# Two graph convolutions: node rows as three exact bfloat16 parts, three bfloat16 products per item, and a ring of 16 slots instead of 24

## The reference, cut to what matters

```python
def _gcn_conv(x, src, dst, W, b):
    h = x * (deg_out ** (-0.5))[:, None]
    h = h @ W
    m = segment_sum(h[src], dst, num_segments=N)
    return m * (deg_in ** (-0.5))[:, None] + b
h = relu(_gcn_conv(layernorm(x), src, dst, W1, b1))
x = x + _layer_norm(_gcn_conv(h, src, dst, W2, b2), gamma, beta)
```

## Time and profile before

| what | value |
|---|---|
| median of 3 runs | 5920.07 us (5916.95 to 5927.35) |
| profiled execution | 5863.58 us |
| its span in the trace | 5861.9 us |
| mean granted clock of TensorE | 0.793 of full |
| busy: PE, PEld, DVE, ACT, POOL | 66%, 48%, 44%, 16%, 50% |
| p1's items, about | 2897 to 4119 us |
| c1's tile loop, about | 4122 to 4189 us |
| p2's items, about | 4204 to 5399 us |

### The profile page before, as it was taken

One profiled execution on the slowest core, in us unless ns is written; L12 is line 12 of the kernel. 1 busy time (PEld: TensorE's weight loads), 2 busy tenths in 40 slices (PEclk: granted clock), 3 DMA queues, 4 the chain that ended last, 5 costly groups with the idle time before them and its releaser, 6 DMA issues.

```text
span 5861.9 us, 62152 instructions
## 1 busy us (share of the span) xinstructions
PE 3845.1 (66%) x14313; PEld 2804.7 (48%) x14313; DVE 2575.1 (44%) x7839; ACT 966.5 (16%) x2299; POOL 2943.7 (50%) x2860
## 2 busy tenths in 40 slices
PE   1666667777788799999355555554655555556368
PEld 0333335566667588888233333333433333334257
DVE  8433234555576511111244444445444444445841
ACT  5333232222102522222200000000200000000421
POOL 0666665565300033333366666667266666664513
PEclk9777778888898799999667767666767776767669
DMA  2333335565687344444433333332233333332202
GB/s 78 106 105 108 105 106 178 185 195 186 198 254 235 107 109 115 111 109 110 140 88 93 91 92 92 92 92 80 81 91 92 92 92 92 92 92 84 88 16 32
DMA packets 322621, 660.17 MB, mean 113 GB/s; under 512 B 60683, under 2 KB 142923, under 8 KB 322150
## 3 DMA queue, kind: packets, MB, share of 16 engines
q0 software_dynamic: 148960, 365.25, 21.4%
q1 hardware_dynamic: 152870, 253.42, 14.4%
q10 hardware_dynamic: 20448, 37.52, 2.1%
HBM read 488.94 MB, written 174.87 MB: 113 GB/s over the span
## 4 chain that ended last, share of the span: by engine, by line
PE 20%; issue 11%; DVE 10%; another core or an unknown queue 6%; DVEq 2%; DMA 1%; ACT 1%; SPq 0%; POOL 0%; POOLq 0%; ACTq 0%
PE bank L1769 15%; DVE reg_b L1313 6%; DVEq L304 2%; PE bank L1717 2%; DVE reg_a L1298 1%; PE bank L1728 1%; PE bank L1689 1%; DVEq L1313 1%; DVE small L822 0%; DVE work L1471 0%; DMA conv_rows<-work 0%; PE bank L1750 0%; DVE work L1505 0%; ACT reg_b L681 0%
## 5 line engine op out<-in xcount | busy, mean ns | idle before, releaser
L1769 PE MATMUL bank<-work,reg_a 128*128 x3520 | 1329.6, 526 | 1175.0 <-issue 626.0
L617 POOL DMA_INDIRECT work<-conv_rows,tables x1662 | 1575.8, 948 | 935.5 <-issue 482.9
L1769 PEld LDWEIGHTS bank<-work,reg_a 128*128 128x128 f32 x3520 | 821.3, 256 | 1683.2 <-issue 1570.1
L1313 DVE TENSOR_TENSOR reg_b<-reg_b,bank 128x257 f32 x1760 | 743.1, 422 | 1026.2 <-remote 518.6
L578 POOL DMA_INDIRECT messages<-work,small x880 | 884.3, 1005 | 536.3 <-ACT work L708 251.2
L1628 PE MATMUL bank<-reg_b,reg_a 128*128 x1760 | 602.8, 477 | 427.6 <-issue 191.1
L1298 DVE TENSOR_SCALAR reg_a<-iota,tables 128x128 f32<-128x128 f32 x1760 | 553.7, 315 | 274.9 <-issue 197.5
L1628 PEld LDWEIGHTS bank<-reg_b,reg_a 128*128 128x128 f32 x1760 | 363.1, 229 | 610.1 <-issue 569.8
L708 ACT ACTIVATE work<-bank,tables 128x256 f32<-128x256 f32 x880 | 397.7, 474 | 1042.5 <-PE bank L1628 630.4
L599 POOL DMA_INDIRECT residual_rows<-work,slot_t x112 | 177.9, 1589 | 478.2 <-DVE work L1282 308.3
L1641 PE MATMUL bank<-reg_b,reg_a 128*128 128x257 f32 x1544 | 395.0, 405 | 28.3 <-DVE reg_a L1164 16.3
(11 more groups left out here) (340 smaller groups left out, 3827.5 us busy)
## 6 DMA issues: line engine op xcount, KB each, us to landing
reg_b<-messages SPq DMA_DIRECT2D x316, 258.0 KB
reg_a<-in_L_ffn_W_dram SPq DMA_DIRECT2D x56, 1024.0 KB, 5.4
reg_a<-item_rows SPq DMA_DIRECT2D x110, 256.0 KB
work<-conv_rows,tables POOLq DMA_INDIRECT x1662
b_rows<-messages ACTq DMA_DIRECT2D x72, 258.0 KB
reg_b<-messages ACTq DMA_DIRECT2D x70, 258.0 KB
b_rows<-messages SPq DMA_DIRECT2D x56, 258.0 KB
messages<-work,small POOLq DMA_INDIRECT x880
```

The costliest lines, as they stand in the source:

```text
L617: g.indirect_dma_start(GC[:, u, 0:D], None, table, bass.IndirectOffsetOnAxis(ap=BSRC[:, b_:b_ + 1], axis=0)).then_inc(z(f"conv_in{u // 4}" ...
L1313: v.tensor_tensor(acc, acc, ps[i % 8][:, 0:D + 1], ALU.add).then_inc(z(f"{tag}_add"), 1)
L1769: pe.matmul(ps[i % 8][:, 0:D + 1], OHP[:, i % (2 * OHN), :], GCf[:, bass.ds(offs[i % 4], D + 1)], start=True, stop=True).then_inc(z(f"{tag ...
```

## The change

Each fp32 number of a row is stored as three bfloat16 numbers that add up to it exactly: its upper 16 bits (the head), the upper 16 bits of what is left (the middle), and what is left then (the rest). A row has 3 x 256 bfloat16 numbers, 1536 bytes instead of 1024, and a slot of the ring has 770 (with the one, and one to pad). The ring has 16 slots. The one-hots are bfloat16 too, made from a bfloat16 copy of the row of column numbers (`IOTAB`). An item is three products into the same bank: rest with the column of ones (257 columns), middle, head (256 each).

The row's producer now writes fp32 to a buffer of its own (`XF`, two chunks), and three copies fill `XR`: ACT copies the heads of a chunk (a strided read of every second 16-bit number, 1792 numbers a partition), DVE subtracts the heads from the numbers (into `XL`) and then the middles from that (the rests), ACT copies the middles from `XL`. SP waits for all three before it writes the chunk. In `c1`, a chunk's heads go at the first tile of the next chunk, its rests at the third, its middles at the fifth; the last chunk's follow the loop, and its rests stand ahead of the zeroing of `ACC`. The semaphores of one-hots, additions and ones are shared by the two convolutions.

```diff
     U = 16
-    UM = UC = 24
+    UM, UC = 24, 16
     NI = -(-(NBLK + T - 1) // U) * U
...
         x2_t = dram("residual_rows", [FPAD, D])
-        conv1_t = dram("conv1_rows", [T * P, D])
-        conv2_t = dram("conv2_rows", [T * P, D])
+        conv1_t = dram("conv1_rows", [T * P, 3 * D], BF16)
+        conv2_t = dram("conv2_rows", [T * P, 3 * D], BF16)
         xn4_t = dram("ffn_in_rows", [T * P, D])
-        WORK = 6700
+        WORK = 6640
+        PARTS = 3 * D
+        SLOT = PARTS + 2
         SMALL = 2600
...
         OHN = 4
-        OHP = ta[:, 0:2 * OHN * P].rearrange("p (s n) -> p s n", n=P)
+        OHP = ta[:, 0:OHN * P].bitcast(BF16).rearrange("p (s n) -> p s n", n=P)
         G, BOH8 = carve(0, UM * W, 2 * 222)
         G = G.rearrange("p (u w) -> p u w", w=W)
-        GCf = work[:, 0:UC * (D + 1)]
-        GC = GCf.rearrange("p (u w) -> p u w", w=D + 1)
+        GCf = work[:, 0:UC * SLOT // 2].bitcast(BF16)
+        GC = GCf.rearrange("p (u w) -> p u w", w=SLOT)
+        assert UC * SLOT // 2 <= WORK
         BOH8 = [BOH8[:, k * 222:(k + 1) * 222].bitcast(BF16)[:, 0:9 * T].rearrange("p (j t) -> p j t", t=T) for k in range(2)]
...
         assert T * D + 3 * QW <= NE * HC * D and QW <= NE * D
-        XR, XT, ZB = carve(0, 2 * CH * D, 2 * D, 2 * D)
-        XR = XR.rearrange("p (s t d) -> p s t d", s=2, d=D)
+        XR, XT, ZB = carve(0, 3 * CH * D, 2 * D, 2 * D)
+        XR = XR.bitcast(BF16).rearrange("p (s t d) -> p s t d", s=2, d=PARTS)
+        XF = ta[:, 0:2 * CH * D].rearrange("p (s t d) -> p s t d", s=2, d=D)
+        XFH = ta[:, 0:2 * CH * D].bitcast(BF16).rearrange("p (s t d k) -> p s t d k", s=2, d=D, k=2)[:, :, :, :, 1]
+        XL = B2B[:, 0:CH * D].rearrange("p (t d) -> p t d", d=D)
+        XLH = B2B[:, 0:CH * D].bitcast(BF16).rearrange("p (t d k) -> p t d k", d=D, k=2)[:, :, :, 1]
+        assert T * (D + 1) + 2 * CH * D <= NE * KC * H and CH * D <= NE * D
         XT = XT.rearrange("p (s c n) -> p s c n", s=2, c=KC)
...
             return z(f"rows_out{k}"), 16 * (before * each + (each if n is None else n))
+        PARTED = dict(p1=0, p2=NCH)
+        def parts_free(tag, c):
+            return rows_out(c % 2, 1 + CONV[tag], c // 2)
         assert EC % 2 == 0
...
             for c in range(NCH):
-                sp.wait_ge(*norms("ln3", "norm", c + 1))
+                for part in ("head", "middle", "rest"):
+                    sp.wait_ge(z(f"part_{part}"), PARTED["p1"] + c + 1)
                 sp.dma_start(nodes(conv1_t, c), XR[:, c % 2, :, :]).then_inc(z(f"rows_out{c % 2}"), 16)
...
                         pool.wait_ge(z(f"{tag}_free"), b_ - UC + 4)
-                    g.indirect_dma_start(GC[:, u, 0:D], None, table,
+                    g.indirect_dma_start(GC[:, u, 0:PARTS], None, table,
                                          bass.IndirectOffsetOnAxis(ap=BSRC[:, b_:b_ + 1], axis=0)
...
             network(**MOE)
+            def heads(tag, c):
+                if c >= 2:
+                    act.wait_ge(*parts_free(tag, c))
+                a.copy(XR[:, c % 2, :, 0:D], XFH[:, c % 2]).then_inc(z("part_head"), 1)
+            def middles(tag, c):
+                act.wait_ge(z("part_left"), PARTED[tag] + c + 1)
+                a.copy(XR[:, c % 2, :, D:2 * D], XLH).then_inc(z("part_middle"), 1)
             for c in range(NCH + 1):
...
                     if c >= 3:
-                        act.wait_ge(*rows_out((c - 1) % 2, 1, (c - 1) // 2))
-                    ln_apply("ln3", c - 1, lambda i: X[:, (c - 1) * CH + i, :], lambda i: XR[:, (c - 1) % 2, i, :])
+                        act.wait_ge(z("part_left"), c - 2)
+                    ln_apply("ln3", c - 1, lambda i: X[:, (c - 1) * CH + i, :], lambda i: XF[:, (c - 1) % 2, i, :])
+                    act.wait_ge(*norms("ln3", "norm", c))
+                    heads("p1", c - 1)
+                if c >= 2:
+                    middles("p1", c - 2)
+            middles("p1", NCH - 1)
             def releases(tag):
...
                 if c >= 2 and t % CH == 0:
-                    act.wait_ge(*rows_out(c % 2, 2, c // 2))
-                a.activation(XR[:, c % 2, t % CH, :], ZB[:, t % 2, :], ACT.Relu, scale=DO[:, t:t + 1]
+                    act.wait_ge(z("part_left"), PARTED["p2"] + c - 1)
+                a.activation(XF[:, c % 2, t % CH, :], ZB[:, t % 2, :], ACT.Relu, scale=DO[:, t:t + 1]
                              ).then_inc(z("relu1"), 1)
+                if c >= 1 and t % CH == 0:
+                    act.wait_ge(z("relu1"), c * CH)
+                    heads("p2", c - 1)
+                if c >= 1 and t % CH == 4:
+                    middles("p2", c - 1)
+            act.wait_ge(z("relu1"), T)
+            heads("p2", NCH - 1)
+            middles("p2", NCH - 1)
             releases("p2")
...
             v.tensor_copy(TRIB[:, 0, :], TRI[:])
+            v.tensor_copy(IOTAB[:], IOTA[:])
             v.memset(TRIB[:, 2, :], 1.0)
...
                         v.wait_ge(z(f"{tag}_mm"), i - 7)
-                    v.tensor_scalar(OHP[:, i % 8, :], IOTA[:], DREL[:, i:i + 1], None, ALU.is_equal
-                                    ).then_inc(z(f"{tag}_oh"), 1)
-                v.memset(GC[:, :, D:D + 1], 1.0).then_inc(z(f"{tag}_one"), 1)
+                    v.tensor_scalar(OHP[:, i % 8, :], IOTAB[:], DREL[:, i:i + 1], None, ALU.is_equal
+                                    ).then_inc(z("conv_oh"), 1)
+                v.memset(GC[:, :, PARTS:PARTS + 1], 1.0).then_inc(z("conv_one"), 1)
                 for i in range(OHN):
...
                     if i:
-                        v.wait_ge(z(f"{tag}_add"), i)
+                        v.wait_ge(z("conv_add"), CONV[tag] * NI + i)
                     acc = ACCf[:, bass.ds(offs[i % 4], D + 1)]
-                    v.tensor_tensor(acc, acc, ps[i % 8][:, 0:D + 1], ALU.add).then_inc(z(f"{tag}_add"), 1)
+                    v.tensor_tensor(acc, acc, ps[i % 8][:, 0:D + 1], ALU.add).then_inc(z("conv_add"), 1)
             v.wait_ge(z("s_add"), NPR)
...
             network(**MOE)
-            for c in range(NCH + 1):
+            def rests(tag, c):
+                n = PARTED[tag] + c
+                if n:
+                    v.wait_ge(z("part_middle"), n)
+                    v.wait_ge(z("part_rest"), n)
+                v.tensor_tensor(XL, XF[:, c % 2], XFH[:, c % 2], ALU.subtract).then_inc(z("part_left"), 1)
+                v.wait_ge(z("part_left"), n + 1)
+                if c >= 2:
+                    v.wait_ge(*parts_free(tag, c))
+                v.tensor_tensor(XR[:, c % 2, :, 2 * D:PARTS], XL, XLH, ALU.subtract).then_inc(z("part_rest"), 1)
+            for c in range(NCH + 2):
                 if c < NCH:
...
                     ln_stats("ln3", c, lambda i: X[:, c * CH + i, :])
-                if c >= 1:
+                if 1 <= c <= NCH:
                     ln_scale("ln3", c - 1, extra=DO)
+                if c >= 2:
+                    v.wait_ge(*norms("ln3", "norm", c - 1))
+                    rests("p1", c - 2)
             v.wait_ge(z("acc1_zero"), 1)
...
             item_sums("p1")
-            v.wait_ge(z("p1_add"), NI)
+            v.wait_ge(z("conv_add"), NI)
             step(v.tensor_scalar(RM, ACC[:, :, D], 1.0, None, ALU.max))
...
                 product("c1", 0, t, ZB[:, t % 2, :], GB1B).then_inc(z("lin1"), 1)
+                c = t // CH - 1
+                if c >= 0 and t % CH == 2:
+                    v.wait_ge(z("relu1"), (c + 1) * CH)
+                    rests("p2", c)
+            v.wait_ge(z("relu1"), T)
+            rests("p2", NCH - 1)
             v.memset(ACCf, 0.0).then_inc(z("acc2_zero"), 1)
...
             item_sums("p2")
-            v.wait_ge(z("p2_add"), NI)
+            v.wait_ge(z("conv_add"), 2 * NI)
             for t in range(T):
...
             def item_products(tag):
-                pe.wait_ge(z(f"{tag}_one"), 1)
+                pe.wait_ge(z("conv_one"), CONV[tag] + 1)
                 def places(i):
                     return (pe.value_load(ROW_N[:, i // 4:i // 4 + 1], min_val=1, max_val=NBLK),
-                            table_offsets(PE_, ROW_C[:, i:i + 4], (UC - 1) * (D + 1)))
+                            table_offsets(PE_, ROW_C[:, i:i + 4], (UC - 1) * SLOT))
                 after = places(0)
...
                         after = places(i + 3)
-                    pe.wait_ge(z(f"{tag}_oh"), i + 1)
+                    pe.wait_ge(z("conv_oh"), CONV[tag] * NI + i + 1)
                     if i >= 8:
-                        pe.wait_ge(z(f"{tag}_add"), i - 7)
-                    pe.matmul(ps[i % 8][:, 0:D + 1], OHP[:, i % (2 * OHN), :], GCf[:, bass.ds(offs[i % 4], D + 1)],
-                              start=True, stop=True).then_inc(z(f"{tag}_mm"), 1)
+                        pe.wait_ge(z("conv_add"), CONV[tag] * NI + i - 7)
+                    for k in (2, 1, 0):
+                        width = D + (k == 2)
```

(17 more changed lines are left out.)

## The result

The changed kernel takes 6047.14 us (median of 4 runs, 6039.5 to 6055.8) and the kernel before 5919.9 (4 runs): +127 us, ratio 1.0219 (95% interval 1.02 to 1.0238). The forecast was 6090, in a range from 5690 to 6330. The number is near; of the four terms in its sum one was right, and errors in the others cancelled. That is luck, and the last sections say where.

A forecast was written before the change was run, and what follows sets the result against it. The prediction took waits in both convolutions, from PE's slow queue, as the bound. Its terms, 62 + 62 + 25 + 22 = +171 us on 5863.6, gave 6035, times 1.0096 about 6090 us, range 5690 to 6330.

The forecast's parts named there:

- Bound: Both convolutions, 1222 and 1194 us: the order of waits decides; PE's own queue is slow, not the supply of gathers.
- formula of items and stretches: Each convolution: 880 items at a normal pace plus 55 slow stretches, 739 + 517 = 1256 us instead of 1194.
- Products and PE's queue: Item loop: three bf16 products gain or break even on PE; its queue grows from 7 to 11 instructions an item.
- pace f: Convolutions: time per item outside slow stretches, taken as 0.84 us, between 0.75 and 0.90; before the change 0.806.
- the number of stretches: Convolutions: slow stretches of PE's queue recur every 16 items, so 55 in each, unchanged by the change.
- 80 to 90: Convolutions: this many POOL waits for a freed quad would show the forecast wrong; it expected about 55.
- the second rival: Convolutions: stretches recur every 112 PE-queue instructions, so 86 each, +353 us a convolution, 6680 in all; chance 0.14.
- the price of a stretch: Convolutions: a slow stretch lasts 10.5 us and passes 1.3 items, so 9.4 us over the normal pace.
- Gathers, ring: Convolutions: 1536-byte rows cost nothing, hidden under consumption at 1256 us; 16 slots cost zero, at most +20 a convolution.
- Parts before p1: Ahead of the first convolution: ACT's copies, less a covered row-write wait, plus the last chunk's end: +25 us (15 to 35).
- Parts before p2: Tile loop between the convolutions: 12 copies at 1.6 us on the path plus a tail of 3: +22 us (8 to 31).
- The port stall: First convolution: PE idles 24.13 us for a one-hot beside POOL's addition; it stays; a small case had it go, 6066.

The follow-up runs named there:

- experiment 4: The changed kernel with only one gather in four, the other slots holding zeros: 5192.86 us.
- experiment 3: The changed kernel with only one of the three products per item, the rests: 6030.47 us.
- the second profile: The kernel before, unchanged, profiled once more on another occasion: 5902.97 us.
- the first profile: The kernel before, unchanged, in the profiled execution that the forecast started from: 5863.6 us.
- experiment 2: The kernel before with a ring of 16 slots instead of 24, fp32 rows and products kept: 5910.13 us against 5921.5, ratio 0.9983.
- (6): The changed kernel, unchanged, on another chip, beside the kernel before there: 5363.57 us against 5300.62, ratio 1.0125.
- thinned kernel: The kernel before with 6.0 instead of 7 instructions of PE's queue an item, same arithmetic: first run 5306.48 us against 5307.0, ratio 1.0001.

## Why the prediction came out near, point by point

**Bound.** "So the ring is full and the consumer is late, not the supply" was half of it. On chip 1 a convolution is POOL's work, 831 gathers and its addition, plus POOL's waits: 807.09 busy and 403.1 idle make up 1210 of p1's 1222 us. That is an account of the time and not yet a cause, since POOL waits for PE. But the slow stretches that I read end in such a wait, and without dense gathers there are none (experiment 4). A formula of items and stretches without POOL in it had no term for that.

**Products and PE's queue.** Right in count (three FUSED_REGOPS, 11 instructions), and the floor of 0.92 us an item in experiment 4 is a little above the forecast's pace f. The step that failed is the number of stretches, "POOL's waits for a freed quad still about 55 a convolution": they were 99 and 101, past the 80 to 90 that the forecast named as a sign of being wrong. The waits came by instructions, every 92 to 106, as the second rival had it. The second failing term is the price of a stretch, 9.4 us over the normal pace: with experiment 4's 810 us for the items of the second convolution alone, its 101 waits leave (1234.4 - 810) / 101 = 4.2 us each, an estimate. The rival failed on the same price. So the forecast's 739 + 517 = 1256 met 810 + 424 = 1234, by errors that nearly cancelled; and since one product instead of three changed the number and not the time (experiment 3), the formula itself isn't how the time comes about. The forecast's p1 and p2 (+62 each) measured +26 and +28 against the second profile, +36 and +40 against the first. (The Trainium skill, "Runtime: NRT & Kernel Launch", "Instruction fetch mechanics", gives blocks of 256 instructions. The queue that carries them made 170 transfers instead of 142, 28 more, and 2 x 880 x 4 = 7040 more instructions are 27.5 blocks; the trace agrees on the size, and the waits, 99, still aren't the blocks.)

**What the +26 and +28 are** is not settled. They aren't the number of products or instructions (experiment 3), nor, with fp32 rows, the ring (2). On the chip without a crawl they are absent (6), and without dense gathers so is the crawl (4). Left are the larger rows, the ring of 16 together with them, the bf16 one-hots and the lower granted clock (0.55 and, with one product, 0.50, instead of 0.70), which no run took apart on chip 1. Against the clock speaks that it costs nothing on chip 3 (0.55 and 0.53, p1 at 1061.1), and that with one product PE's quick pace was higher and the time the same.

**Gathers, ring.** Right for the gather, 948 ns at 1536 bytes as at 1024. Nothing for 16 slots is shown with fp32 rows on chip 1 (experiment 2), and with the larger rows only on chip 3 (6).

**Parts before p1.** +25, measured 25.7, and 25.2 on chip 3. The copies took 1.68 us instead of 2.03 and waited 1.6 us for row writes, which the sum had as covered.

**Parts before p2.** +22, measured 43.5, above the bound of 31. The mis-sized term is "Of the 12 copies in the loop I take 1.6 us each on the path, 19": DVE's two subtractions, 4.05 us a chunk, got no price of their own (29 us fit in DVE's idle time), and the loop grew by 39.4 us, nearly the 44 of all four operations. The tail of 3 was 4.6: the 2.57 us of idle ahead of the memset stayed, and the last subtractions came on top.

**The sum.** The convolutions were about 70 too dear against the second profile and the tile loop 21 too cheap. Against the first profile, which the sum starts from, the convolutions were 48 too dear; with the tile loop's 21 that left the sum 27 too high, and 6035 met 6039.5 only because the stretch up to the third normalisation, untouched, took 32.7 us more in that execution. On chip 3 the forecast of the convolutions would have been wrong altogether: the change costs +63 us in all there, the parts alone.

**The port stall**, as the forecast calls PE's long wait beside POOL's addition, stayed: a bf16 one-hot took 22.5 us there, an fp32 one 24.9.

## What to carry to other kernels

When one engine's queue crawls, lay its timeline beside every other engine's before giving the stretch a fixed price: here the stretches that were read ended in a pause of POOL, and right after its pauses hardly any slow instruction began (9 of 299); the time was POOL's work plus its waits. In a loop that hands tiles between engines two deep, a block of work on either engine can go on the path nearly in full (39.4 of 44 us here), however idle both are on average; count it as the length of the block, not against the idle share. Compare a kernel on more than one chip before explaining a wait: the theories here were about something that three other chips don't show.

## What the runs showed of the hardware that was not expected

The same kernel takes 5920 us on one chip and 5299 to 5307 on three others. Some 320 us of that are the two convolutions (1223.8 and 1194.5 against 1061.3 and 1032.3 in the thinned kernel on chip 2), and some 240 lie ahead of the third normalisation, which begins at 2843.0 against 2601.1; there, in the message stage, PE's FUSED_REGOPS take 42 ns at most on both chips, so the crawl isn't all that differs. On the one chip, FUSED_REGOPS of 37 ns in PE's queue take up to 1.41 us while POOL issues a gather every 1.25 us; on the three others, in the thinned kernel, none of 1760 takes over 47 ns. The number of POOL's waits follows the instructions of PE's queue (one for 92 to 106, at 5, 7 and 11 an item), and POOL's idle time doesn't: 401 to 413 us in a convolution of the kernel before, 440 to 447 with the changed rows, for one product or three. Why the chips differ no run here shows.
